# A wait between the quarters of a block's fetched expert matrices, on SyncE's queue

## What is computed

```
# layer 3 of the chain: two linear maps with relu, plus a shared and a per-row
# low-rank correction; every one of the 128 rows has its own expert id in 0..7
hidden_i  = x @ wi.T + 2 * (x @ common_wi_a.T) @ common_wi_b.T + expert_lora(x, id, experts_wi_a, experts_wi_b)
hidden_i  = relu(hidden_i)                                  # 512 wide
hidden_o  = hidden_i @ wo.T + 2 * (hidden_i @ common_wo_a.T) @ common_wo_b.T
hidden_o += expert_lora(hidden_i, id, experts_wo_a, experts_wo_b)
x = x + hidden_o
# layer 4: gelu MLP whose last 32 output columns come from one of 16 experts
```

## Time and profile before

| | us |
|---|---|
| median of 3 runs | 275.11 (273.94 to 278.18) |
| the profiled execution's own time | 276.42 |
| its span, first to last instruction | 274.5 |
| TensorE busy in it | 242.4 |
| VectorE busy | 199.0 |
| granted TensorE clock, mean | 0.988 |

### The profile page before, as it was taken

The page is one execution under the profiler, slowest core; times in us unless marked ns, Lnnn a source line. Parts: engine busy times, 40 slices in busy tenths (PEclk is TensorE's granted clock), DMA queues, the critical chain, the costliest instruction groups (busy, mean ns, idle before and its releaser), DMA issues.

```text
span 274.5 us, 13858 instructions
## 1 busy us (share of the span) xinstructions
PE 242.4 (88%) x5418; PEld 179.8 (66%) x5418; DVE 199.0 (73%) x384; ACT 133.7 (49%) x226; POOL 116.8 (43%) x225
## 2 busy tenths in 40 slices
PE   1949788689996999999999999999999988999876
PEld 1634344457674886688668866886688666668745
DVE  2957688999795758995999599959995897460031
ACT  3235753435293236743674367436743682536031
POOL 6893464159545332353235323532353334410340
PEclk9999999979999799999999999999999999999999
DMA  7998127577487307771776177717774773178401
GB/s 213 387 272 268 46 68 221 179 222 221 142 238 237 123 5 227 224 208 68 228 219 214 65 225 220 218 63 229 222 205 133 239 227 127 33 210 241 138 38 41
DMA packets 36113, 48.77 MB, mean 178 GB/s; under 512 B 11361, under 2 KB 16226, under 8 KB 35954
## 3 DMA queue, kind: packets, MB, share of 16 engines
q1 hardware_dynamic: 35168, 47.17, 56.4%
q10 hardware_dynamic: 914, 1.17, 1.3%
HBM read 44.13 MB, written 4.19 MB: 176 GB/s over the span
## 4 chain that ended last, share of the span: by engine, by line
PE 45%; issue 17%; DVE 15%; POOL 10%; SPq 5%; DMA 3%; POOLq 2%; ACT 2%; ACTq 0%; DVEq 0%
PE pB L799 9%; PE pB L750 5%; PE pB L754 5%; PE pB L832 5%; PE pB L751 5%; POOL sc L399 3%; PE pV L740 3%; DVE sc L1135 3%; PE pV L746 3%; SPq L281 3%; PE pX L690 2%; SPq L282 2%; DVE kb L1128 2%; PE pX L725 2%; DMA cols_s<-cols_dram 2%
## 5 line engine op out<-in xcount | busy, mean ns | idle before, releaser
L425 POOL COPY rw<-e3t_s 128x128 f32 x128 | 39.0, 305 | 52.3 <-issue 41.9
L399 POOL TENSOR_TENSOR sc<-sc,rmax 128x512 f32<-128x512 f32 x32 | 33.6, 1049 | 64.5 <-DVE rmax L1138 64.5
L832 PE MATMUL pB<-rw,hT 128*32 128x128 f32 x960 | 33.2, 276 | 3.6 <-issue 3.5
L534 ACT ACTIVATE ex<-sc 128x512 f32<-128x512 f32 x32 | 20.1, 629 | 24.6 <-POOL sc L399 24.3
L832 PEld LDWEIGHTS pB<-rw,hT 128*32 128x32 f32 x960 | 24.9, 109 | 9.7 <-issue 9.7
L799 PE MATMUL pB<-rw,hT 128*32 128x128 f32 x896 | 27.4, 274 | 0.0
L538 ACT ACTIVATE hT<-pB 128x512 f32<-128x512 f32 x28 | 16.6, 597 | 21.2 <-PE pB L754 21.2
L1128 DVE TENSOR_SCALAR kb<-pX,bqk,cols_s 128x512 f32<-128x512 f32 x32 | 24.3, 801 | 3.5 <-PE pX L754 3.5
L750 PE MATMUL pB<-x_h,ffn_h 128*128 128x512 f32 x50 | 22.2, 443 | 3.4 <-DVE x_h L1189 2.4
L799 PEld LDWEIGHTS pB<-rw,hT 128*32 128x32 f32 x896 | 23.7, 110 | 1.7 <-issue 0.8
L1144 DVE STREAM_TRANSPOSE pt<-ex 128x512 f32<-128x512 f32 x32 | 22.4, 699 | 3.3 <-ACT ex L534 3.1
(11 more groups left out here) (198 smaller groups left out, 509.2 us busy)
## 6 DMA issues: line engine op xcount, KB each, us to landing
rw<-w_d SPq DMA_DIRECT2D x128, 256.0 KB, 3.0
rw<-fc2t_dram SPq DMA_DIRECT2D x4, 768.0 KB, 9.0
w_d<-rw SPq DMA_DIRECT2D x4, 512.0 KB, 3.3
out_dram<-o_s SPq DMA_DIRECT2D x7, 256.0 KB, 2.7
xT<-xt_dram SPq DMA_DIRECT2D x6, 256.0 KB, 2.8
xN<-xn_dram SPq DMA_DIRECT2D x6, 256.0 KB, 2.7
e3t_s<-e3t_dram SPq DMA_DIRECT2D x1, 1024.0 KB, 9.8
ffn_s<-ffn_w_dram SPq DMA_DIRECT2D x1, 896.0 KB, 7.7
```

The source lines that it names most:

```text
L399: pool.tensor_tensor(sc[:, g % 2, :, :], sc[:, g % 2, :, :], rmax[:, g % 2, :].unsqueeze(2).to_broadcast([P, H, S]), ALU.subtract).then_in ...
L425: pool.tensor_copy(rw[:, r, :, SHARED:D], e3t_s[:, bass.ds(e, 1), :, :].rearrange("p o c n -> p (o c) n"))\
L832: last = mm(ps[S * q:S * q + S, P * g:P * g + P], hT[:, c, tok], rw[:, Q4 * g + q, c, :], start=(c == 0), stop=(c == FC - 1))
```

## The change

In `expert_weights2`, on SyncE, a second wait is added for the quarters 1 to 3 of every block: before its four matrices are issued, the four of the quarter ahead must all have landed. Nothing else differs; the lines below move down by two, so that line 281 is 283 in the changed kernel and 282 is 284.

```diff
             def expert_weights2(i, g):
 
                 at(sp, ffo_ps, G * (i - 1) + g + 1)
+                if g > 0:
+                    at(sp, ld_rw2[g - 1], 16 * Q4 * (i + 1))
                 for r in range(Q4 * g, Q4 * g + Q4):
                     e = sp.value_load(e2i[0:1, bass.ds(ROWS * i + r, 1)], min_val=0, max_val=E2 - 1)
                     sp.dma_start(rw2[:, r, :, :].rearrange("p c d -> p (c d)"),
```

## The result

The changed kernel takes 304.88 us (median of 4 runs, 304.53 to 306.57) against 274.52 for the kernel before (4 runs, 273.90 to 278.18). Its profiled execution took 304.53 us, with a span of 302.6.

What follows compares the result with a forecast made beforehand. SyncE's fetch issuing was taken to bound the uncovered ends, with a 4.4 us cushion in the loop. 7.0 + 8.6 + 7.8 + 3.4 + 0.8 = 27.6 on 276.4 makes 304.0, less 1.3 gives 302.7 us; range 292 to 311.

Steps and rivals of the forecast that it cites:

- The boundary: Between quarters SyncE waits 3.0 us for the landing, then 0.72 to issue: 2.6 us more each, 7.8 a block.
- the first rival: At each boundary, a lone quarter's last fetch lands sooner, in 2.6 us: 295 us in total, chance 0.18.
- Block 0: Start of kernel, no cover: 7.8 us show, less 0.75 for a slow landing that may not recur, 7.0.
- Block 1: Fetched in step 2: slack as in the loop plus block 0's delay, which moves the reader too, 0.
- Blocks 2 to 5: Read in steps 3 to 6: first 3.4 us late, next three steps 1.7 more each, 8.6 in all.
- SyncE's 29.2: In the loop: SyncE's own step, 27.46 - 6.1 + 7.8 = 29.2 us, which the reader can't beat.
- The even chance for one more fall: First late step of the loop, 3.4 us of gap: may bring another clock fall, priced at 0.8.
- Block 6: Fetches don't wait for a pooling, read after step 7's other matmuls; cushion larger than 7.8: 0.
- Block 7: In the tail SyncE is the chain, with no cover: 7.8 us.
- The clock: TensorE falls to half clock behind long gaps at block 0 and the tail, 1.7 us each, 3.4; loop 0.8.
- the slow boundary (3.1): Rival: at every boundary landings take 3.5 us as in block 7, costing 3.1 each; 312 us, chance 0.10.
- the clock falling in every late step: Rival: in the loop, four late steps at 1.7 us in place of 0.8 add 6.0; 309 us, chance 0.15.

Runs made afterwards that it cites:

- e2: Changed kernel with the added wait at block 0 alone: 285.09 us against 275.76 for the kernel before, 1.039.
- e11: Changed kernel with the added wait at block 1 alone: 280.00 us against 276.56 for the kernel before, 1.011.
- e1: Changed kernel with the added wait at block 7 alone: 286.94 us against 275.76 for the kernel before, 1.042.
- e5: Changed kernel, but ahead of quarters 2 and 3 SyncE waits for the quarter before the last one: 275.36 us against 275.26 before, 0.999.
- e10: Kernel before, no added wait, with `final(6, 2)` put ahead of `out2(7, 3)` on TensorE: 275.72 us against 274.94, 1.001.
- e7: Changed kernel with each wait one matrix later, behind a quarter's first matrix: 286.36 us against 275.26 for the kernel before, 1.037.
- e9: Changed kernel plus unread matmuls in the tail's gaps, 16 before `out2(7, 2)`, 24 before `out2(7, 3)`: 305.42 us, 1.115 of before.
- e6: Changed kernel with one boundary a block, ahead of quarter 2, not three: 282.05 us against 275.26 for the kernel before, 1.028.
- e3: Changed kernel with the added wait at blocks 2 to 5 alone, fetched in the loop: 284.41 us against 275.76 before, 1.030.

## Why the prediction was right

The forecast of 302.7 us lies 2.2 below the measured 304.88, and the range held it. In the two traces the sum of 27.6 stands against 28.1; the other 1.7 us come from which runs stand for the kernels: the forecast took off 1.3 because the traced run of before lay above its median, and the traced run of after lies 0.35 below its own. The mechanism was right: SyncE's stall at three boundaries, shown in full at the uncovered ends and held back in the loop. That the sum came out within 0.5 is in part luck, since the rows of the table above are off by -0.6, -3.1, +0.9, +1.0 and +2.2. Step by step:

- **The boundary.** Forecast 3.72 us outside the loop and 3.8 in it, in place of 1.13 and 1.19. From the issue of a quarter's last matrix to that of the next quarter's first, the trace after has 3.7 in the loop and 4.1 outside it (means of 12), where before had 1.25 and 1.19. That is 2.5 and 2.9 more, 2.7 in the mean of both, where 2.6 was forecast. A quarter's last fetch did not land in 2.6 us: the median of those that a boundary waits for is 2.96 after, 2.98 before. So the first rival fell on its one premise. The estimate of 2.6 from the Trainium skill (DMA: Bandwidth & Descriptors, Anatomy of one DMA), whose fit is for transfers that GpSimd issues and not SyncE, agrees only with the fetches that are issued with nothing in flight, 2.7 in the median; a quarter's last mostly has two others ahead of it.
- **Block 0.** 7.0 forecast, 6.4 in the trace pair and 9.3 in the time of e2, which includes the clock; 7.0 + 1.7 was right to 0.6. Part of this is luck: the premise that block 0 has no cover holds in the trace of before alone (1.7 to 4.5 us in six others), and its boundaries cost 8.3 to 10.3 us and not 7.8. The two errors nearly cancel.
- **Block 1.** Forecast 0, and 0 in the changed kernel, for the stated reason that its reader is late too. Without that it costs (e11): the slack "as in the loop" would not have done alone.
- **Blocks 2 to 5.** The first late step was 3.48 us, forecast 3.4. The three behind it were forecast at 1.7 of waiting each and waited 0, 2.8 and 0. Their length was near the forecast for another reason in the steps without a wait: the fall of the clock behind each wait stretches the next step from 27.47 to 29.12 us, and in this time the next fetches land. That this equals SyncE's 29.2 is a coincidence. The forecast that SyncE has no idle time left held behind the fetches of blocks 2 and 4 and failed behind those of block 3, where it waited 2.2 us. The even chance for one more fall became two falls.
- **Block 6.** 0 forecast; in the trace after, it had used up its whole cushion of 10.6 us: `out2(6, 3)` started 0.04 us behind the landing. Its three boundaries took 3.62, 4.87 and 5.28 us, 10.0 more than before and not 7.8, since the landings ahead of the last two took 4.1 and 4.5 us; the last of all took 3.9.
- **Block 7.** 7.8 forecast, 8.8 measured from `out2(5, 3)` to `out2(7, 3)`. Step 7 was 0.7 us shorter in this stretch, and from `out2(6, 0)` on it is 9.6: 8.0 for the three boundaries, 1.6 for slower issues within the quarters, and 0.6 because SyncE, still issuing block 6's last matrices, came late to block 7, less 0.6 for a quicker last landing. In e1, where block 6 has no wait, it is 7.6.
- **The clock.** This is the mis-sized term, and the step that was off is the number of falls in the tail, not the price of one: 1.7 us were forecast for one fall, and 3.9 measured behind `out2(7, 3)`. There were two, here in the changed kernel (columns as in the earlier trace rows):

```profile
276.00:288.00 12.00, 6.74 (x112) 5.25 (x108) 0.00 (x0) 0.60 (x1) 0.33 (x2) 0.50 0.32 89
288.00:291.00 3.00, 1.12 (x29) 0.83 (x22) 1.90 (x4) 0.00 (x0) 1.44 (x5) 0.95 0.13 50
292.00:295.00 3.00, 3.00 (x8) 2.31 (x7) 0.00 (x0) 1.54 (x3) 1.31 (x2) 0.50 0.00 0
```

From `out2(7, 3)` to the end, the kernels whose trace has no fall there take 15.6 to 15.8 us (before, e2 to e5, e10). e7 has the first fall alone, behind a wait of 5.24 us, and takes 17.5; e11 has the second alone, and so has e9, and they take 17.3 and 17.0. Both make 18.8 in e6 and 19.7 in e1 and the changed kernel. The tail of e7, and then that of e11:

```profile
264.00:270.00 6.00, 3.10 (x60) 2.89 (x64) 0.00 (x0) 0.60 (x1) 0.00 (x0) 0.50 0.28 80
271.00:284.00 13.00, 8.88 (x178) 6.80 (x176) 3.65 (x8) 3.35 (x5) 3.36 (x9) 1.00 0.13 42
```

```profile
260.40:266.00 5.60, 3.73 (x101) 3.10 (x102) 1.99 (x4) 0.60 (x1) 1.74 (x6) 1.00 0.08 33
267.00:270.00 3.00, 3.00 (x8) 2.33 (x8) 0.00 (x0) 1.45 (x3) 1.59 (x3) 0.50 0.00 0
```

So a fall alone cost 1.4 to 1.9 us, as priced. The second one follows an idle time of TensorE of some 2 us that the tail has with or without the change, among them. It came in six of the seven traces with a stall at block 7 (not in e7) and in one of the seven without (e11). So it goes with the stall, but neither needs it nor always follows it, and why is open.

Of the rivals, the slow boundary (3.1) and the clock falling in every late step were each partly true: outside the loop 2.9, and both waits in the loop did bring their fall. They cost less than worked out, because a step either waits or runs behind a fall, by turns.

## What to carry to other kernels

When a queue only waits and issues, add up its own list for one round of the loop before adding a wait to it: here the step followed 27.46 - 6.1 + 2.6 n to within 0.9 us for n = 4 and 7 waits, where SyncE never idled between its rounds, and to within 1.2 us for n = 3, where it still did in one step. A wait for a landing in the issuing queue costs the landing time and the 0.7 us from the release to the next issue, less one issue interval, here 2.5 to 2.9 us each time, and it is free only up to the slack; read that slack from several traces where a single one has an odd step. Where the reader is TensorE, price the gap at more than its length.

## What was not expected

- A stall of 2.8 us in the tail came with 3.1 more through the clock (e6), one of 7.6 with 3.9 (e1), but the 5.24 us wait of e7 with only 1.9. In these three what set the price was whether the clock fell once or twice, and how long it stayed down, and the length of the gap did not tell which.
- One trace can mislead more than once: the 1.4 us "given back" in step 2, the 8.5 us cushion of block 1 and the missing cover of block 0 all came from one trace. Its step 2 was some 2 us longer than in the traces of e1, e3 and e5 and had a fall of the clock, at 90 us, that theirs have not.
- The stalls change little in the transfers themselves: with none and with three boundaries a block the median landing stayed at 2.9 to 3.0 us, and what is quicker is the one fetch issued with nothing in flight.
